# An attention and expert kernel on one core: PSUM banks, the order of rows, transfers and threshold steps rearranged, and products without a use put on TensorE around the boundary of its two programs

## The chip, the core and the metric

The kernel runs on one core of a Trainium2 chip. The metric is the device time of one execution in microseconds (us). The engines of the core are named as the profile names them: PE is TensorE (PEld its weight loads), DVE is VectorE, ACT is ScalarE, POOL is GpSimd, SP is SyncE, which here only starts transfers. Each engine runs its own list of instructions in order; semaphores join them.

## The reference, cut to what matters

```
xn  = layernorm(x)                                   # x: 2 x 4096 x 512, so 8192 rows of 512
qkv = xn @ qkv_w + qkv_b                             # in windows of 64 rows, 16 heads of 32
p   = softmax(q @ k.T / sqrt(32) + rel_bias)         # 64 x 64 for each window and head
att = (p @ v) @ proj_w + proj_b
scores = (xn @ Wg.T).T                               # 8 experts x 8192 rows
top_vals, token_idx = top_k(scores, 1024)            # for each expert
token_w = softmax(top_vals)
h   = silu(xg @ W1.T) * (xg @ W3.T)                  # xg = xn[token_idx], 1024 x 512, hidden 1024
y   = (h @ W2.T) * token_w
out = x + att + scatter_add(y at token_idx)
```

## The kernel before

The kernel is two programs, one after the other. `attention_block` makes layernorm, attention, the gate scores and the choice of 1024 rows for each expert. `expert_block` runs the eight experts. Every large product is made three times over (`split3`, lines 59 to 61: high by high, high by low, low by high parts, each 128 x 128 by 512 columns), and twelve such products make one 128 x 512 result.

The attention program goes over 16 chunks of 512 rows (c = 0 to 15, T = 512, G = 4 groups of four heads, s = 4c + g). Its order is written out by hand for every engine. On PE a chunk is: q and k of group 0, the tiles 0 and 1 of v, pv (line 918) of a group of the chunk before, scores (line 852) of group 0; q and k of group 1, v tiles 2 and 3, pv, scores of group 1; q and k of group 2, `project_out` tile 0 of the chunk before, the gate product of the next chunk (line 832), `project_out` tiles 1 and 2, pv, scores of group 2; `project_out` tile 3, q and k of group 3, pv, scores. Below, out0 to out3 are the four tiles of `project_out`, v0 to v3 those of v, and T0 is the start of a chunk's first q product.

A group's softmax goes round four engines: DVE adds the bias to the scores and takes the maximum (`add_bias`, lines 1203 and 1208), POOL subtracts it (482), ACT takes the exponential (633), DVE sums (1212) and inverts (1216), POOL multiplies (498), DVE turns 32 x 32 blocks (`turn_probs`, 1255), ACT copies (`own_blocks`, 629), SP moves the other blocks (`spread_probs`, 377), and PE reads them in pv. ACT also copies q and k out of PSUM (613 and 638), DVE copies v (`v_part`, 1268).

The next chunk's rows are loaded (`load_x`, 571), normed on DVE (`layernorm_stats`, 1155; `layernorm_apply`, 1174; the square root is POOL's line 468), stored (`keep_xn`, 576), loaded back in another layout (`load_back`, 388) and turned on DVE (`turn_blocks`, 1180); the gate product reads them. In chunks 4 to 9 the five last chunks' rows go the same way ahead of time (the names with `_ahead`: 593, 597, 405, 1185, 838). `finish_rows` (1221) adds `project_out` to the residual rows `x_res`, which `load_res` (588) loads and `store_out` (581) stores.

PSUM has eight banks. Scores take 0 to 3, pv takes 4 and 5, q takes 6 (QB), k takes 7 (KB). v and `project_out` have no banks of their own: they go where `V_BANK` and `P_BANK` say.

Chunks 10 to 14 (`hunt_chunk`) also look for the threshold of each expert, two bits of a float's order at a time in 16 rounds: `search` (1308, then `threshold_float` 1292 and 1293, then three comparisons 1312 and 1313), a product (943) and `take_bits` (1298 to 1304). Chunk 13 chooses (`choose`, 1332), chunk 14 makes places and weights, chunk 15 makes the first expert's list (products 157).

## Time and profile before

| | |
|---|---|
| runs | 2065.02, 2067.38, 2062.08 us, median 2065.02 |
| the profiled execution | 2066.15 us, its span 2064.3 us |
| PE busy in the span | 1961.5 us (95%), mean granted clock 0.977 |
| DVE, ACT, POOL busy | 1185.0, 648.7, 600.9 us |
| chunks 1 to 9 | 68.07 to 600.85 us |
| chunks 10 to 15 | 600.85 to 957.04 us |
| the end of the first program and the start of the second | 957.04 to 991.30 us |
| the experts | 991.30 to 2064.3 us |

The rows of the trace, in a section below, are read like this. A row of the timeline has a start, a duration, engine, line, operation and the names it writes and reads; in brackets stands how long the engine sat idle before it and what ended that. "<-issue" is idle time with no cause that the profile shows. PEclk is the clock that TensorE was granted, 1.00 for 2.4 GHz and 0.50 for 1.2 GHz. Matmuls overlap, so one of 512 columns reads 0.39 us while the next one starts 0.227 us after it, and at half clock reads 0.63 us while the next starts 0.427 us after it.

### The profile page before, as it was taken

What the parts mean: (1) busy time and instruction counts of PE and PEld (TensorE: products, weight loads), DVE (VectorE), ACT (ScalarE), POOL (GpSimd) and SP (SyncE); (2) the same over time, 40 slices, a digit from 0 to 9 for tenths busy, and PEclk for the clock granted to TensorE, in tenths of its full rate; (3) what the DMA queues carried; (4) which work ended last, traced back from release to release, by engine and by line L of the source; (5) the groups of instructions that cost most, each with busy time, mean ns of one, the idle gap of its engine ahead of it and who ended that gap; (6) DMA issues with size and microseconds to landing.
All of it is one profiled execution on the core that took longest, in us unless ns stands there. A gap on an engine that the chain in (4) does not pass through costs nothing.

```text
span 2064.3 us, 39324 instructions
## 1 busy us (share of the span) xinstructions
PE 1961.5 (95%) x16627; PEld 1575.6 (76%) x16627; DVE 1185.0 (57%) x1688; ACT 648.7 (31%) x953; POOL 600.9 (29%) x410
## 2 busy tenths in 40 slices
PE   7899989899998899988899999999999999999997
PEld 5677767677777777776688888888888888888886
DVE  6666668677768898776744544345344543444221
ACT  3333333232333343332333242233332333323221
POOL 1444445444344443454122021211212112102111
PEclk9999999999999999999999999999999999999999
DMA  6333355566542222323444253233532434325311
GB/s 188 111 113 111 105 168 140 140 180 168 146 131 67 58 63 78 84 68 103 154 108 107 81 133 92 55 110 88 128 83 62 126 82 104 91 70 142 61 21 21
DMA packets 170612, 213.63 MB, mean 103 GB/s; under 512 B 31712, under 2 KB 103776, under 8 KB 170464
## 3 DMA queue, kind: packets, MB, share of 16 engines
q1 hardware_dynamic: 124976, 116.12, 20.4%
q0 software_dynamic: 14336, 33.56, 9.1%
q10 hardware_dynamic: 31152, 61.87, 8.7%
q8 instruction: 106, 1.74, 0.4%
q14 instruction: 42, 0.34, 0.1%
HBM read 127.08 MB, written 51.38 MB: 86 GB/s over the span
## 4 chain that ended last, share of the span: by engine, by line
PE 49%; DVE 1%; SPq 1%; ACT 0%; DMA 0%; issue 0%; POOL 0%; POOLq 0%
PE ps_e L59 16%; PE ps_e L60 16%; PE ps_e L61 16%; SPq L197 1%; PE ps_e L157 0%; DMA raw<-in_w 0%; ACT w_hi L1737 0%; DVE w_lo L1848 0%; DVE x_f L145 0%; DVE xn L1854 0%; POOL out_rows L1701 0%; DVE hm L1880 0%; DVE xgt_lo L1859 0%; DVE hot_v L136 0%; ACT x_res L1769 0%
## 5 line engine op out<-in xcount | busy, mean ns | idle before, releaser
L59 PE MATMUL ps_e<-xgt_hi,w_hi 128*128 128x512 f32 x1024 | 404.3, 395 | 7.7 <-DVE xgt_lo L1859 7.7
L61 PE MATMUL ps_e<-xgt_hi,w_lo 128*128 128x512 f32 x1024 | 399.0, 390 | 0.0
L60 PE MATMUL ps_e<-xgt_lo,w_hi 128*128 128x512 f32 x1024 | 399.0, 390 | 0.0
L1880 DVE TENSOR_TENSOR hm<-ps_e,silu 128x512 f32<-128x512 f32 x128 | 88.5, 691 | 457.2 <-PE ps_e L61 456.4
L59 PEld LDWEIGHTS ps_e<-xgt_hi,w_hi 128*128 128x128 f32 x1024 | 192.5, 188 | 46.5 <-DVE xgt_lo L1859 8.4
L1701 POOL DMA_INDIRECT out_rows<-x_res,idx x64 | 100.6, 1572 | 428.1 <-ACT x_res L1769 413.7
L61 PEld LDWEIGHTS ps_e<-xgt_hi,w_lo 128*128 128x128 f32 x1024 | 192.6, 188 | 40.5
L60 PEld LDWEIGHTS ps_e<-xgt_lo,w_hi 128*128 128x128 f32 x1024 | 192.9, 188 | 38.1
L186 POOL DMA_INDIRECT x_in<-xn_rows,idx x64 | 80.1, 1252 | 481.3 <-DVE idx L178 307.5
L59 PE MATMUL ps<-xt_hi,wqk_hi 128*128 128x512 f32 x512 | 209.2, 409 | 4.1 <-DVE v_sb L1268 1.8
L60 PE MATMUL ps<-xt_lo,wqk_hi 128*128 128x512 f32 x512 | 203.4, 397 | 3.9 <-issue 3.9
L61 PE MATMUL ps<-xt_hi,wqk_lo 128*128 128x512 f32 x512 | 202.3, 395 | 0.7 <-issue 0.7
L1757 ACT ACTIVATE h_hi<-hm 128x512 fp32r<-128x512 f32 x128 | 81.0, 633 | 387.7 <-DVE hm L1880 384.8
L59 PE MATMUL ps_e<-w_hi,h_hi 128*128 128x512 f32 x512 | 199.3, 389 | 0.6 <-DVE got L165 0.6
L60 PE MATMUL ps_e<-w_lo,h_hi 128*128 128x512 f32 x512 | 199.2, 389 | 0.0
L61 PE MATMUL ps_e<-w_hi,h_lo 128*128 128x512 f32 x512 | 199.2, 389 | 0.0
L498 POOL TENSOR_TENSOR pn_sb<-p_sb,s_rec 128x1024 f32<-128x1024 f32 x62 | 119.2, 1922 | 260.9 <-DVE s_rec L1216 196.6
L482 POOL TENSOR_TENSOR s_sb<-s_sb,s_max 128x1024 f32<-128x1024 f32 x64 | 122.8, 1919 | 211.5 <-DVE s_max L1208 211.5
L1866 DVE TENSOR_TENSOR h_lo<-hm,h_hi 128x512 fp32r<-128x512 f32 x128 | 88.6, 692 | 94.6 <-ACT h_hi L1757 91.5
L629 ACT ACTIVATE pt<-pn_sb 128x1024 f32<-128x1024 f32 x62 | 65.7, 1060 | 237.2 <-DVE pn_sb L1255 231.1
L1255 DVE STREAM_TRANSPOSE pn_sb<-pn_sb 128x1024 f32<-128x1024 f32 x62 | 77.1, 1243 | 84.3 <-POOL pn_sb L498 83.7
L1769 ACT ACTIVATE x_res<-ps_e,weight 128x512 f32<-128x512 f32 x64 | 43.0, 690 | 251.0 <-PE ps_e L61 251.0
(188 smaller groups left out, 3471.6 us busy)
## 6 DMA issues: line engine op xcount, KB each, us to landing
x_f<-in_w SPq DMA_DIRECT2D x48, 512.0 KB
raw<-in_w SPq DMA_DIRECT2D x48, 512.0 KB
x_res<-in_x ACTq DMA_DIRECT2D x16, 1024.0 KB, 8.7
xn<-x_in SPq DMA_DIRECT2D x256, 64.0 KB, 2.0
pt<-pn_sb SPq DMA_DIRECT2D x248, 64.0 KB
out_rows<-x_res ACTq DMA_DIRECT2D x15, 1024.0 KB
xn_rows<-xt_plain ACTq DMA_DIRECT2D x9, 1024.0 KB, 4.2
x_in<-xn_rows SPq DMA_DIRECT2D x28, 256.0 KB, 4.2
```

Source lines behind the costliest of these rows:

```text
L59: nc.tensor.matmul(out, w_hi, x_hi, start=start, stop=False)
L60: nc.tensor.matmul(out, w_hi, x_lo, start=False, stop=False)
L61: return nc.tensor.matmul(out, w_lo, x_hi, start=False, stop=stop)
L186: nc.gpsimd.indirect_dma_start(out=k.x_in[:, t, :], out_offset=None, in_=xn_rows, in_offset=bass.IndirectOffsetOnAxis(ap=k.idx[par][:, til ...
L482: nc.gpsimd.tensor_tensor(s_sb[:, :, :, :], s_sb[:, :, :, :], s_max[:, :].rearrange("p (t h) -> p t h", t=TT).unsqueeze(3) .to_broadcast([ ...
L498: nc.gpsimd.tensor_tensor(halves_first(pn_sb[:, :]), p_sb[:, :, :, :].rearrange("p t h (j c) -> p (t h) j c", c=QD), s_rec[:, :].unsqueeze ...
L629: nc.scalar.activation(pt[s % 2][:, :, :, :, :].rearrange("p i t h q -> p (i t h q)"), pn_sb[:, :], ACT.Copy).then_inc(pt_own, 1)
L1255: nc.vector.transpose(blocks, blocks).then_inc(pn_turned, 1)
L1701: nc.gpsimd.indirect_dma_start(out=d["out"], out_offset=bass.IndirectOffsetOnAxis(ap=lists.idx[par][:, tile0 + t:tile0 + t + 1], axis=0), ...
L1757: nc.scalar.activation(h_hi[:, m, :], hm[:, m % 2, :], ACT.Copy).then_inc(h_hi_ready, 1)
L1866: v.tensor_tensor(h_lo[:, m, :], hm[:, m % 2, :], h_hi[:, m, :].bitcast(F32), ALU.subtract).then_inc(h_ready, 1)
L1880: v.tensor_tensor(hm[:, m % 2, :], ps[:, 2 * (m % 2) + 1, :], silu[:, m % 2, :], ALU.mult).then_inc(hm_ready, 1)
```

## The change

It has five parts.

1. Banks. `V_BANK` and `P_BANK` become QB, KB, QB, KB. v0 to v3 and out0 to out3 no longer touch the scores' banks 0 and 1. So v tiles wait for the copy of q or k that was in the bank, out0 and out1 likewise, and out2 and out3 wait for `finish_rows` of out0 and out1. Scores wait neither for `v_part` nor for `finish_rows`. What follows in QB or KB (the next q and k) waits for `v_part`.
2. Rows. On DVE `layernorm_stats` goes ahead of `normaliser(s - 1)` and `layernorm_apply` ahead of `v_part(c, 1)`. `turn_blocks` goes ahead of `add_bias(s + 1)`, all of `turn_blocks_ahead` behind it. `gate_rows` goes ahead of `turn_probs(s + 1)`, and `gate_rows_ahead` and `layernorm_stats_ahead` behind the third `finish_rows`. POOL's `layernorm_rstd` goes ahead of `normalise(s - 1)`. PE's `gate_ahead` goes behind out2. In chunks 10 to 14 two of the four `turn_blocks` go behind `take`.
3. Transfers. `load_res`, `keep_xn`, `keep_xn_ahead` and `load_x_ahead` go from ACT's queue to SP's. `load_x` stays on ACT and is issued at the end of the chunk before.
4. Thresholds. The key is kept as the float's own bits, so `threshold_float` (two instructions) is needed once, not in each of 16 rounds and in `choose`, which also loses a copy.
5. Products without a use: 16 behind the last `probs_t` and 12 behind the last `pv`, each 128 x 256, and 26 of 128 x 128 in full float ahead of the first expert. Nothing reads them.

The diff, cut to its core:

```
-        V_BANK, P_BANK, FINAL_BANK = (0, KB, 0, KB), (0, 1, QB, KB), (0, 1, 2, 3)
+        V_BANK, P_BANK, FINAL_BANK = (QB, KB, QB, KB), (QB, KB, QB, KB), (0, 1, 2, 3)
...
                 spread_probs(s - 2)
+                load_res(c - 1)
...
                 if FAR < j <= NCH:
-                    load_back_ahead(j - 1)
+                    keep_xn_ahead(j - 1)
+                if n < FAR:
+                    keep_xn(n)
                 spread_probs(s - 1)
                 if n < NCH:
                     load_back(n)
+                if FAR < j <= NCH:
+                    load_back_ahead(j - 1)
                 spread_probs(s)
+                if j == FAR:
+                    sp.wait_ge(xn0_stored, 2 * 16 * TT * NQ)
+                if FAR <= j < NCH:
+                    load_x_ahead(j)
...
                 subtract_max(s - 1)
-                normalise(s - 1)
                 if n < FAR:
                     layernorm_rstd(n)
+                normalise(s - 1)
...
                 k_part(s + 3, 3)
+                if c + 2 < FAR:
+                    load_x(c + 2)
...
             def project_v(c, t):
-                if t % 2:
-                    pe.wait_ge(k_ready, G * c + t // 2 + 1)
-                elif G * c + t // 2 >= 1:
-                    pe.wait_ge(s_ready, G * c + t // 2)
+                pe.wait_ge(k_ready if t % 2 else q_ready, G * c + t // 2 + 1)
...
                 if t == 0:
                     pe.wait_ge(o_ready, s)
-                    pe.wait_ge(s_ready, s + 2)
-                elif t == 2:
                     pe.wait_ge(q_ready, s + 3)
-                elif t == 3:
+                elif t == 1:
                     pe.wait_ge(k_ready, s + 3)
+                else:
+                    pe.wait_ge(out_ready, TT * c + t - 1)
...
                 pv(s - 2, 2)
-                pe.wait_ge(v_ready, TT * c + 1)
                 slot_read(c, 1)
                 scores(s)
+                pe.wait_ge(v_ready, TT * c + 1)
                 project_q(s + 1, 1)
...
                 lists_of(6)
+                if ahead:
+                    gate_ahead(j - 1)
                 pv(s, 0)
                 lists_of(7)
-                pe.wait_ge(out_ready, TT * (c - 1) + 2)
...
+            def idle_products(n, bank):
+                for _ in range(n):
+                    nc.tensor.matmul(ps[:, bank, 2 * P:4 * P], wqk_hi[:, 0, 0, :], wv_hi[:, 0, 0:2 * P], start=True, stop=True)
...
                 probs_t(s + 3)
+                idle_products(16, OT)
                 pv(s + 3, 3)
+                idle_products(12, PT)
                 pe.wait_ge(o_ready, G * NCH)
...
             def search(i):
-                then(v.scalar_tensor_tensor(cand[:, :], pattern[:, :], 30 - 2 * i, key[:, 0:1].to_broadcast([P, 3]),
-                                            ALU.logical_shift_left, ALU.bitwise_or))
-                threshold_float()
+                then(v.scalar_tensor_tensor((thr if i else cand)[:, :], pattern[:, :], 30 - 2 * i, key[:, 0:1].to_broadcast([P, 3]),
+                                            ALU.logical_shift_left, ALU.bitwise_xor))
+                if i == 0:
+                    threshold_float()
...
-                turn_blocks(c + 1, *range(KC))
+                turn_blocks(c + 1, 0, 1)
                 take(c, 4)
                 if choosing:
                     take_room(SLOT)
                     choose_ties()
+                turn_blocks(c + 1, 2, 3)
...
+            for _ in range(26):
+                nc.tensor.matmul(ps[:, LISTS, 0:P], lists.ident[:, :], lists.ident[:, :], start=True, stop=True)
             expert(0)
```

Three places show what the order becomes. DVE in the first half of chunk 3, before (s_sb is the bias, ot_lo the low part of pv's result, s_sum and s_rec the normaliser, pn_sb the turned probabilities):

```order
133 L1212 TENSOR_REDUCE s_sum<-p_sb 128x16 [waits exp_ready]
134 L1216 RECIPROCAL s_rec<-s_sum 128x16 [waits norm_ready,sum_ready]
135 L1268 TENSOR_TENSOR v_sb<-ps,v_bias 128x512 [waits v_mm,o_mm]
136 L1255 STREAM_TRANSPOSE pn_sb<-pn_sb 128x1024 [waits norm_ready]
137 L1268 TENSOR_TENSOR v_sb<-ps,v_bias 128x512 [waits v_mm]
138 L1155 BN_STATS stats<-x_in 128x6 [waits x_loaded]
139 L1155 BN_STATS stats<-x_in 128x6 x3
140 L1160 BN_AGGR mv<-stats 128x2 [waits stat_ready]
141 L1160 BN_AGGR mv<-stats 128x2 x3
142 L1163 TENSOR_SCALAR veps<-mv 128x4 [waits mv_ready]
143 L1203 TENSOR_TENSOR s_sb<-ps,rel 128x4x4x64 [waits exp_ready,s_mm]
```

and now:

```order
133 L1158 BN_STATS stats<-x_in 128x6 [waits x_loaded]
134 L1158 BN_STATS stats<-x_in 128x6 x3
135 L1163 BN_AGGR mv<-stats 128x2 [waits stat_ready]
136 L1163 BN_AGGR mv<-stats 128x2 x3
137 L1166 TENSOR_SCALAR veps<-mv 128x4 [waits mv_ready]
138 L1215 TENSOR_REDUCE s_sum<-p_sb 128x16 [waits exp_ready]
139 L1219 RECIPROCAL s_rec<-s_sum 128x16 [waits norm_ready,sum_ready]
140 L1271 TENSOR_TENSOR v_sb<-ps,v_bias 128x512 [waits v_mm,o_mm]
141 L1258 STREAM_TRANSPOSE pn_sb<-pn_sb 128x1024 [waits norm_ready]
142 L1177 TENSOR_SCALAR xt_plain<-x_in,mv,rstd 128x4x4x32 [waits rstd_ready]
143 L1177 TENSOR_SCALAR xt_plain<-x_in,mv,rstd 128x4x4x32 x3
144 L1271 TENSOR_TENSOR v_sb<-ps,v_bias 128x512 [waits v_mm]
```

The statistics moved ahead of the normaliser and the norming ahead of the copy of v1. SP's queue over one chunk with rows ahead, before:

```order
109 L377 DMA pt<-pn_sb 32x512 [waits pt_own]
110 L377 DMA pt<-pn_sb 32x512 x3
111 L405 DMA x_f<-xn_rows 32x16x128 [waits xnf_stored]
112 L405 DMA x_f<-xn_rows 32x16x128 x3
113 L377 DMA pt<-pn_sb 32x512 [waits pt_own]
114 L377 DMA pt<-pn_sb 32x512 x3
115 L388 DMA x_in<-xn_rows 32x16x128 [waits xn_stored]
116 L388 DMA x_in<-xn_rows 32x16x128 x3
```

and now:

```order
106 L377 DMA pt<-pn_sb 32x512 [waits pt_own]
107 L377 DMA pt<-pn_sb 32x512 x3
108 L385 DMA x_res<-in_x 128x4x512 [waits out_stored]
109 L394 DMA xn_rows<-xt_f 128x4x512 [waits xnf_ready]
110 L399 DMA xn_rows<-xt_plain 128x4x512 [waits xn_ready]
111 L377 DMA pt<-pn_sb 32x512 [waits pt_own]
112 L377 DMA pt<-pn_sb 32x512 x3
113 L409 DMA xn<-xn_rows 32x16x128 [waits xn_stored]
114 L409 DMA xn<-xn_rows 32x16x128 x3
115 L426 DMA x_f<-xn_rows 32x16x128 [waits xnf_stored]
116 L426 DMA x_f<-xn_rows 32x16x128 x3
```

Three transfers of ACT's stand between the first two spreads now, and the load back of the rows ahead stands behind the load back of the next chunk. PE at the end of the first program, now (before, the two rows of 128x256 and the one of ps_e<-ident are not there):

```order
3419 L897 MATMUL ps<-ident,pn_sb 128x128 [waits ptb_ready,pta_ready,norm_ready]
3420 L897 MATMUL ps<-ident,pn_sb 128x128 x7
3421 L1111 MATMUL ps<-wv_hi,wqk_hi 128x256 x16
3422 L915 MATMUL ps<-pt,v_sb 32x64 [waits o_ready,ptb_ready,pta_ready]
3423 L915 MATMUL ps<-pt,v_sb 32x64 x31
3424 L1111 MATMUL ps<-wv_hi,wqk_hi 128x256 x12
3425 L59 MATMUL ps<-wp_hi,ot_hi 128x512 [waits o_ready]
```

The products stand ahead of the instruction that waits, so they run while it would wait.

## Rows read from the trace of the kernel before

**Rows 1.** Stretches: us, busy us (instructions) of each engine, PEclk, DMA share, GB/s.

```profile
68.07:600.85 532.78, 497.50 (x6455) 384.79 (x6449) 374.98 (x541) 162.46 (x216) 241.74 (x158) 0.96 0.48 139
600.85:957.04 356.19, 328.77 (x4282) 264.12 (x4276) 287.73 (x457) 129.73 (x215) 156.10 (x98) 0.96 0.27 78
...
991.30:2064.30 1073.00, 1061.62 (x5051) 870.69 (x5049) 452.50 (x598) 322.38 (x475) 172.80 (x121) 1.00 0.37 90
```

**Rows 2.** Chunks, the same view: 1, 6, 7, 11 and 13.

```profile
68.07:123.75 55.68, 52.73 (x718) 41.58 (x713) 36.84 (x51) 18.01 (x24) 26.19 (x17) 1.00 0.37 116
...
356.11:421.68 65.57, 58.23 (x727) 43.95 (x721) 45.99 (x69) 18.06 (x24) 27.38 (x18) 0.92 0.52 148
...
421.68:479.40 57.72, 55.72 (x727) 42.82 (x721) 45.54 (x69) 18.13 (x24) 27.41 (x18) 0.97 0.59 168
...
661.89:722.80 60.91, 55.66 (x706) 44.68 (x704) 52.79 (x95) 23.99 (x44) 25.52 (x16) 0.94 0.26 71
...
782.37:842.45 60.08, 55.94 (x721) 44.84 (x716) 50.25 (x87) 21.40 (x36) 24.64 (x16) 0.94 0.26 72
```

**Rows 3.** Waits of PE in chunks 1 to 15: total us, times, longest.

```profile
PE ps L852 <- DVE x_res L1221: 15.7, 5, 4.4
PE ps L832 <- DVE xt_plain L1180: 13.7, 6, 4.8
PE ps L59 <- ACT k_sb L638: 13.3, 8, 1.9
```

**Rows 4.** Timeline of chunk 7 up to the turned rows.

```profile
421.64 0.53 ACTq L571 DMA_DIRECT2D x_in<-in_x  x1
...
424.63 0.68 DVE L1273 TENSOR_TENSOR ot_lo<-ps,ot_hi 128x512 fp32r<-128x512 f32 x1
...
427.82 1.22 DVE L1212 TENSOR_REDUCE s_sum<-p_sb 128x16 f32<-128x1024 f32 x1 [2.51 <-ACT p_sb L633]
...
432.07 1.91 POOL L498 TENSOR_TENSOR pn_sb<-p_sb,s_rec 128x1024 f32<-128x1024 f32 x1 [5.38 <-DMA pt<-pn_sb]
...
435.75 2.45 DVE L1155 BATCH_NORM_STATS2 stats<-x_in 128x6 f32<-128x512 f32 x4
...
441.79 3.12 DVE L1174 TENSOR_SCALAR xt_plain<-x_in,mv,rstd 128x512 f32<-128x512 f32 x4
...
444.94 0.37 ACTq L576 DMA_DIRECT2D xn_rows<-xt_plain  x1
...
444.98 0.50 PE L59 MATMUL ps<-wv_hi,xt_hi 128*128 128x512 f32 x1 [1.89 <-ACT k_sb L638]
...
457.01 2.49 DVE L1180 STREAM_TRANSPOSE xt_plain<-x_in 128x512 f32<-128x512 f32 x4 [2.52 <-DMA x_in<-xn_rows]
```

**Rows 5.** Timeline of chunk 6: the gate product.

```profile
399.63 1.94 PE L832 MATMUL ps<-xt_plain,wg 128*32 128x512 f32 x8 [4.78 <-DVE xt_plain L1180]
```

**Rows 6.** Timeline of chunk 11, DVE and PE around scores of group 2.

```profile
701.36 1.75 DVE L1293 SCALAR_TENSOR_TENSOR thr<-cand,flip 128x3 int32<-128x3 int32 x1
...
703.14 2.88 DVE L1312 TENSOR_SCALAR x_f<-x_f,thr 128x512 bf16<-128x512 f32 x2
...
706.61 0.68 DVE L1221 TENSOR_TENSOR x_res<-ps,x_res 128x512 f32<-128x512 f32 x1
...
709.07 1.28 PE L852 MATMUL ps<-k_sb,q_sb 32*64 32x64 f32 x64 [4.39 <-DVE x_res L1221]
```

**Rows 7.** Line 1293: duration ns min/median/max, first and last start.

```profile
L1293 DVE SCALAR_TENSOR_TENSOR thr<-cand,flip x17: 161/163/1746, 620.6 to 809.1; 128x3 int32<-128x3 int32 x17
```

**Rows 8.** Timeline of the boundary: PE.

```profile
973.10 0.85 PE L918 MATMUL ps<-pt,v_sb 64*32 64x64 f32 x64 [2.20 <-ACT pt L620]
...
975.36 0.80 PE L59 MATMUL ps<-wp_hi,ot_hi 128*128 128x512 f32 x1 [1.41 <-DVE ot_lo L1273]
...
988.58 0.79 PE L59 MATMUL ps_e<-xgt_hi,w_hi 128*128 128x512 f32 x1 [7.73 <-DVE xgt_lo L1859]
```

**Rows 9.** Transfers of 60 to 960 us: count, KB each, median us to landing.

```profile
x_in<-in_x ACTq DMA_DIRECT2D x5, 1024.0 KB, 7.8
```

90 lines of the change are left out of this document (38 added, 52 removed).

## The prediction, made before the changed kernel ran

> **What bounds the kernel now.** I read the stretches first, then the chunks, then PE's waits, then the timeline around the waits. The experts run from 991.30 us to the end with PE busy in 1061.62 of 1073.00 us at full clock, and the change only puts products ahead of them [rows 1]. So all that can move lies ahead of 991 us. There PE is the engine that the others wait for, but it has holes. In chunks 1 to 9 it is busy 497.50 of 532.78 us, in chunks 10 to 15 328.77 of 356.19 [rows 1]: 35.3 and 27.4 us idle. A part of the busy time is work at half clock as well. Chunk 1, all of it at clock 1.00, has 52.73 us of PE work [rows 2]. Nine of these are 474.6 us, the five gate products ahead add 1.06 us each, and 17.6 of the 497.5 us are left: that is what 1.2 GHz costs there. Six times 52.7 from 328.8 leaves 12.6 us in chunks 10 to 15. So holes and half clock together are 93 us, the most the change could give but for the boundary.
>
> Three waits make most of the holes [rows 3]: scores behind `finish_rows` (15.7 us, 5 times, in the chunks from 10 on), the gate product behind `turn_blocks` (13.7 us, 6 times) and v3 behind the copy of k (13.3 us, 8 times, once in each chunk from 1 to 9 but one). The change takes away all three as they stand. What counts is which wait ends last in its place.
>
> **Chunks 1 to 9, first half of a chunk.** I follow chunk 7, T0 = 421.68, and count from T0. Now the rows are loaded from 421.64 (T0+0) [rows 4]; the statistics begin at 435.75 (T0+14.1), so `add_bias` of group 0 behind them is late, and with it the maximum, the subtraction, the exponential and the copy of k: v3 starts at 444.98 (T0+23.3) after 1.89 us of waiting. In the change the statistics stand behind `ot_lo`, whose instruction ends at T0+3.6 [rows 4]. They can't begin sooner than that, and not before the rows are there. The load goes out up to a microsecond sooner and a median one lands after 7.8 us [rows 9], beside another megabyte that now starts later. So they begin between T0+3.6 and T0+7; I take T0+5.5, between the two. They take 3.0 us. The normaliser had its exponential at 427.82 (T0+6.1) [rows 4], needs 1.5 us, and now ends at T0+8.1 to 11.5 (10.0). POOL's multiplication began at T0+10.4 since it waited 5.38 us for the spread [rows 4]; the spread is now ahead of the residual's load, so POOL goes by the normaliser, 1.9 us, to T0+12.0. The turning of the probabilities takes 1.25, `layernorm_apply` 3.12, the copy of v1 0.65: T0+17 (15.2 to 18.6). k of group 1, next in bank KB, wants it at T0+15.5. **New wait one: 0 to 3.1 us, I take 1.4.** From the copy of v1 on, `add_bias`, maximum, subtraction, exponential and copy of k take 6.1 us as before; v3 starts at T0+23.1 (21.3 to 24.7), where it is 23.3 now. So the wait of 1.9 us is cut into two of 1.4 and about 0.6, and nothing is won but the clock: chunk 7 has 55.72 us of busy time [rows 2] where 52.73 and 1.06 would do. The 1.9 us over are v3's, whose products ran at 1.2 GHz behind the hole.
>
> **Second half of a chunk.** From the store of the normed rows (444.94) to the turned ones (457.01) the way is 12.1 us [rows 4]. The norming now ends at T0+16.4, so they are back at T0+28.5, and DVE has copied v3 at about T0+26.6. `turn_blocks` (2.5), `add_bias` and maximum (2.4) and `ot_lo` (0.7) now stand ahead of out0, which gets its input at T0+34.1. PE wants it 10 us behind v3's start (v3, pv, scores, q, k): at T0+33.1. **New wait two: about 0.9 us.** For that the gate product waits for nothing, where it waited 4.78 us in chunk 6 [rows 5] and 13.7 in all. out1 and out2 find k copied and out0 finished with 0.5 to 2 us to spare. In chunks 4 to 8 `layernorm_stats_ahead` (3.0 us) now stands ahead of `add_bias` of group 2, and its rows can't be loaded before `turn_blocks_ahead`, now late in the chunk: between 0 and 2 us each, 0.6 taken. Sum of the nine chunks: idle 9 x 2.9 + 5 x 0.6 = 29 us, and 4 us of fetches and spreads stay: 33 for 35.3, so **2 us**. The new holes are each below 1.9 us, the size behind which chunk 7 ran v3 slowly; a hole of 1.04 us in chunk 1 left the clock at 1.00 [rows 2]. So nearly all of the 17.6 us of half clock goes; I take **17**. Bounds for the stretch: -4 (each new wait at its upper end, clock as now) and +38.
>
> **Chunks 10 to 15.** In chunk 11 the last search ahead of `finish_rows` has an instruction of three numbers (line 1293) that takes 1.75 us, and two comparisons that take 2.88 [rows 6]; line 1293 has a median of 0.16 us [rows 7]. They stretch while POOL works. `finish_rows` of out0 runs at 706.61 to 707.3, of out1 0.6 us behind the next turning, and scores start at 709.07 after 4.39 us [rows 6]. In the change out2 (2.73 us) waits for out0's, and scores come 3.6 us behind it. With `finish_rows` where it is, scores would be later by 1.8 us. But each search loses two instructions, between 0.35 us (two at 0.17) and some 2.5 us (two behind a POOL instruction), and the last two searches of the chunk add up. I take 2.8 us sooner: scores 1.0 us sooner, and 0.7 us less waiting ahead of the small products. With that 2 us for each of the chunks 10 to 12, **6 us**. The hole stays above 3 us, so does its half clock. Chunk 13's choice loses three such instructions, in the trace 1.2 us each beside POOL's residual, which held up the copy of v3 and through it PE by 1.75 us, and a later wait of 2.2 us with its half clock: **5 us** of its 60.08 against 52.7 [rows 2]. Chunk 15: scores no longer wait for v0, **1 us**. Together 12, between 0 and 20.
>
> A row here speaks of a cost that may not leave. The comparisons right behind line 1293 are themselves stretched, 2.88 us for the two [rows 6]. If they are what would wait next, the search gets only the 0.17 us of each instruction back: `finish_rows` comes 1.3 instead of 2.8 us sooner, and these three chunks lose what they won: 2030 becomes 2036. The Trainium skill says so (SBUF — State Buffer, section on the two separate sides): a VectorE instruction that uses the port pair shared with GpSimd blocks fully until GpSimd's instruction ends. That is a rival below.
>
> **The boundary.** PE waits 2.20 us, then 1.41, then 7.73 [rows 8]; between the last two, out0 to out3's last 12 products run from 975.36 at 0.427 us each, and the first seven of the experts too. A product of 256 columns is half of 0.227 us: 16 are 1.8 us, 12 are 1.4, hidden in the first two holes. The 26 are of full float like the gate product, whose four, of 512 columns and side by side, take 1.06 us at full clock: with 128 columns one takes 0.27 us at most, all 7.0 us, hidden in 7.73. If the clock stays up, 12 x 0.2 and 7 x 0.2 us go: **4 us**. At half clock the 26 take up to 14 us and hold the experts up by up to 6.
>
> **The sum.** 2 + 17 + 12 + 4 = 35. The profiled execution took 2066.15 us (span 2064.3), so 2031.2; the median of the runs is 1.1 lower, so 2030.
>
> **Rivals.**
> 1. *The holes only move* (0.20). The new wait for v1's copy, out0's and out2's wait are near their upper ends and the clock drops behind them. Against it: each is short by the rows. Then chunks 1 to 9 give 5, 10 to 15 give 4, the boundary 4: 2053.
> 2. *The rows come late* (0.06). All of the first half now hangs on the load of x: each us past T0+5.5 costs one in each of nine chunks. At T0+9.4 the 35 us are gone; at T0+10.5, as late as with two other megabytes in flight, the kernel stands at 2030 + 45 = 2075, slower.
> 3. *The blocked time passes on* (0.14), as said: 2036.
> 4. *The products don't keep the clock* (0.10): the 26 delay the experts by up to 6 us, say 4, instead of winning 4: 2038.
> 5. *More goes* (0.10). If the load lands at T0+3.6, wait one and most of two vanish too: 9 x 2 us more, 2012.
>
> The forecast has 0.40. The range of 2010 to 2056 takes in the first rival and the fifth, and leaves out the second and the tails. About 0.3% (6 us) can be told from no change. Faster by more than that has 0.90, within it 0.05, slower 0.05.
>
> **What would show it.** In the changed profile: scores behind `finish_rows`, the gate product behind `turn_blocks` gone from PE's waits; products with wqk behind a copy of v about 12 us in all; wp products behind `ot_lo` about 8 us; out2 behind `finish_rows` 3 to 4 us in each of three chunks; PEclk 1.00 in most of chunks 1 to 9; PE full from 970 us on with no product at 0.63 us. Wrong would be: statistics that wait for the load past T0+7, or a clock that falls behind holes of 1.4 us.

## The result: 2006.7 us, 58.7 less, and more than the forecast had

| | before | changed |
|---|---|---|
| median of the runs shown | 2065.41 us (2062.08 to 2067.38) | 2006.71 us (2006.31 to 2008.94) |
| ratio | | 0.972, 95% interval 0.9703 to 0.9736 |
| span of the profiled execution | 2064.3 us | 2004.5 us |
| PE busy, mean granted clock | 1961.5 us, 0.977 | 1946.2 us, 0.992 |

The forecast was 2030, with 2010 to 2056 as its range. The direction was right and the size was not: the time lies 3 us below the range.

The stretches of the changed kernel come first, cut at the same places in the program as [rows 1], but for the last cut, which is the first product of the experts here (930.25 us, and 988.58 us before). The columns are those of [rows 1].

```profile
67.07:554.59 487.52, 481.65 (x6454) 376.57 (x6449) 368.51 (x541) 160.41 (x216) 241.95 (x158) 1.00 0.53 152
554.59:901.85 347.26, 324.06 (x4281) 260.03 (x4275) 276.63 (x426) 130.15 (x215) 156.10 (x98) 0.98 0.28 80
901.85:930.25 28.40, 25.80 (x342) 22.02 (x337) 21.65 (x28) 9.23 (x14) 12.16 (x9) 1.00 0.43 137
930.25:2004.50 1074.25, 1062.90 (x5056) 871.56 (x5056) 455.02 (x601) 322.81 (x475) 173.50 (x123) 1.00 0.37 91
```

For the kernel before, the last two with the same cut (PE's time only):

```profile
957.04:988.58 31.54, 18.99 (x262) 0.83 0.39 122
988.58:2064.30 1075.72, 1064.34 (x5056) 0.99 0.37 91
```

| stretch | before | changed | gain | forecast |
|---|---|---|---|---|
| up to chunk 1 | 68.07 | 67.07 | 1.0 | 0 |
| chunks 1 to 9 | 532.78 | 487.52 | 45.3 | 19 |
| of it PE busy (half clock) | 497.50 | 481.65 | 15.9 | 17 |
| of it PE idle | 35.28 | 5.87 | 29.4 | 2 |
| chunks 10 to 15 | 356.19 | 347.26 | 8.9 | 12 |
| boundary and experts | 1107.26 | 1102.65 | 4.6 | 4 |

So one term holds the whole miss: the idle time of PE in chunks 1 to 9. I had written 33 us for it in the changed kernel, and it is 5.9. (One execution is not exact to the microsecond. `idle_only`, an experiment below whose program is that of the kernel before in these chunks, takes 539.8 us for them where the row of the kernel before has 532.8; three experiments with the changed kernel's program in them take 487.2 to 487.6.) The waits of PE in these chunks are now (total us, times, longest), where [rows 3] had 13.7 and 13.3 us:

```profile
PE ps L59 <- issue: 2.7, 2, 2.3
PE ps L59 <- ACT k_sb L648: 1.2, 5, 0.3
PE ps L60 <- issue: 0.9, 1, 0.9
```

None of the new waits that I had put there shows: no product with wqk waits for a copy of v (12 us were said), none with wp waits for `ot_lo` (8 us).

**Chunk 7 of the changed kernel** answers [rows 4]; T0 is 386.87. Line numbers have moved a little: statistics 1158, applying 1177, copy of v 1271, turning 1183.

```profile
385.26 0.39 ACTq L602 DMA_DIRECT2D x_in<-in_x  x1
...
392.62 2.47 DVE L1158 BATCH_NORM_STATS2 stats<-x_in 128x6 f32<-128x512 f32 x4 [0.22 <-DMA x_in<-in_x]
...
399.20 1.25 DVE L1258 STREAM_TRANSPOSE pn_sb<-pn_sb 128x1024 f32<-128x1024 f32 x1 [1.47 <-POOL pn_sb L529]
400.37 1.88 DVE L1177 TENSOR_SCALAR xt_plain<-x_in,mv,rstd 128x512 f32<-128x512 f32 x4
402.16 0.69 DVE L1271 TENSOR_TENSOR v_sb<-ps,v_bias 128x512 f32<-128x512 f32 x1
...
402.27 0.36 SPq L399 DMA_DIRECT2D xn_rows<-xt_plain  x1
...
402.93 0.47 PE L59 MATMUL ps<-xt_hi,wqk_hi 128*128 128x512 f32 x1
...
413.62 2.48 DVE L1183 STREAM_TRANSPOSE xt_plain<-x_in 128x512 f32<-128x512 f32 x4
...
418.37 0.68 DVE L1276 TENSOR_TENSOR ot_lo<-ps,ot_hi 128x512 fp32r<-128x512 f32 x1
```

Read it against the prediction's walk, in us from T0. The statistics begin at 5.75 (I had 5.5). The turned probabilities are done at 13.6 (13.2). Applying takes 1.88 us, where I had 3.12 from [rows 4], so it ends at 15.4 and the copy of v1 at 16.0 (17). PE asks for that bank at 16.06 (15.5): it comes 0.1 us too late to wait. The turned rows are not waited for either: `turn_blocks` starts as the copy of v3 ends, at 26.7 (28.5), and `ot_lo` is done at 32.2 (34.1), where out0 starts (33.1). Not every link was shorter: the first ones ended 0.3 to 0.4 us later than I had. But applying took 1.2 us less and PE asked 0.6 us later, and together that is the 1.4 us of the first forecast wait. out0 was asked for 0.9 us sooner than I had, and its input was there 1.9 us sooner.

**Chunks 10 to 12** have the new hole that the prediction named. The waits stand ahead of out1 and out2, here in chunk 10 (the next eight products start 0.33 to 0.59 us apart, at half clock):

```profile
592.59 0.50 PE L59 MATMUL ps<-wp_hi,ot_hi 128*128 128x512 f32 x1 [1.68 <-ACT k_sb L648]
...
598.61 0.79 PE L59 MATMUL ps<-wp_hi,ot_hi 128*128 128x512 f32 x1 [2.96 <-DVE x_res L1224]
```

And what `finish_rows` stands behind on DVE, with POOL's rows beside it:

```profile
593.68 3.61 DVE L1320 TENSOR_SCALAR x_f<-x_f,thr 128x512 bf16<-128x512 f32 x2
593.70 1.91 POOL L529 TENSOR_TENSOR pn_sb<-p_sb,s_rec 128x1024 f32<-128x1024 f32 x1 [2.83 <-DVE s_rec L1219]
595.56 5.33 POOL L538 TENSOR_TENSOR xt_lo<-xt_plain,xt_hi 128x512 fp32r<-128x512 f32 x4
597.21 0.73 DVE L1321 TENSOR_SCALAR_CACHE_REDUCE x_f<-x_f,thr 128x512 bf16<-128x512 f32 x1
...
597.87 0.68 DVE L1224 TENSOR_TENSOR x_res<-ps,x_res 128x512 f32<-128x512 f32 x1
```

**The boundary** answers [rows 8]: the idle products fill the holes, and the first product of the experts starts 0.06 us behind the end of `xgt_lo`.

```profile
919.43 0.50 PE L59 MATMUL ps<-wp_hi,ot_hi 128*128 128x512 f32 x1
...
924.12 6.04 PE L1840 MATMUL ps_e<-ident 128*128 128x128 f32 x52 [1.67 <-PEq L208]
...
927.63 2.56 DVE L1866 TENSOR_TENSOR xgt_lo<-xn,xgt_hi 128x512 fp32r<-128x512 f32 x4
930.25 0.50 PE L59 MATMUL ps_e<-xgt_hi,w_hi 128*128 128x512 f32 x1
```

### The profile page after: what moved, and what is told of

It reads as the page before. It is cut to its first block, busy times and chain, and to the rows that moved or that the text cites. A ratio compares the mean times of both kernels' runs of the same rounds, so it can differ in the third digit from the quotient of the medians.

```text
span 2004.5 us, 39470 instructions
## 1 busy us (share of the span) xinstructions
PE 1946.2 (97%) x16707; PEld 1569.4 (78%) x16707; DVE 1166.6 (58%) x1657; ACT 647.1 (32%) x953; POOL 599.5 (30%) x410
## 3 DMA queue, kind: packets, MB, share of 16 engines
q1 hardware_dynamic: 143456, 152.82, 26.7%
## 4 chain that ended last, share of the span: by engine, by line
PE 51%; DVE 1%; ACT 1%; SPq 0%; DMA 0%; issue 0%; POOL 0%; POOLq 0%
PE ps_e L59 17%; PE ps_e L61 17%; PE ps_e L60 17%; PE ps_e L157 1%; SPq L197 0%; DMA raw<-in_w 0%; ACT w_hi L1742 0%; DVE w_lo L1855 0%; DVE x_f L145 0%; DVE xn L1861 0%; POOL out_rows L1706 0%; DVE hm L1887 0%; DVE xgt_lo L1866 0%; DVE hot_v L136 0%; ACT x_res L1774 0%
## 5 line engine op out<-in xcount | busy, mean ns | idle before, releaser
L59 PE MATMUL ps<-wp_hi,ot_hi 128*128 128x512 f32 x256 | 106.5, 416 | 15.2 <-DVE x_res L1224 9.7
```

The costliest lines, as they stand in the source:

```text
L59: nc.tensor.matmul(out, w_hi, x_hi, start=start, stop=False)
```

## The experiments

Fifteen kernels, each the changed kernel or the kernel before with one or two edits. "Changed" is 2006.7 us. Each was run beside the kernel before, and the ratio given is to that. The intervals of the ratios are 0.4 to 1.2% wide, 4 to 13 us each way, and no experiment ran beside the changed kernel itself, so a difference from "changed" that is smaller than that rests on the waits and stretches of the profiles. The stretches of an experiment are cut where a chunk starts, as before.

### Two links made longer

`apply_plus`:

```diff
...
                 dve.wait_ge(rstd_ready, c + 1)
+                for t in ((0, 1) if c >= 2 else ()):
+                    nc.vector.tensor_reduce(idle_sum[:, 2 * c + t:2 * c + t + 1], v_bias[:, :], AX.X, ALU.add)
```

> The changed kernel with two sums over the bias of v (about 0.6 us each on DVE, results unused) ahead of layernorm_apply in chunks 1 to 8: what the applying would take if it were stretched as in the kernel before (3.12 instead of 1.88 us). In the changed kernel the copy of v1 ends 1.5 to 1.8 us ahead of the product of k that waits for its bank in chunks 1 to 4, and 0.06 to 0.4 us ahead in chunks 5 to 9. Theory A, the gain is there because this chain comes out just short: about 1 us of new waiting in each of chunks 5 to 8 and none in 1 to 4, so 4 us and up to 4 more of half clock, 2011 (2010 to 2015). Rival, the chain has slack that the profile doesn't show: 2006 to 2008.

Measured: 2012.6 us (ratio 0.9741, 0.9696 to 0.9786), 5.9 us more. The interval holds the changed kernel's 0.972, but all four runs lie above all four of the changed kernel, and chunks 1 to 9 take 496.0 us instead of 487.5. The sums run in nine chunks, 1 to 9, not in eight as the expectation has it (18 sums, of 0.66 us each at the median). The products with wqk now wait for the copy of v, 3.8 us in 5 times, the longest 1.1.

`load_late`:

```diff
                 o_hi_part(s - 3, 1)
+                if c + 1 < FAR:
+                    load_x(c + 1)
                 own_blocks(s - 2)
...
-                if c + 2 < FAR:
-                    load_x(c + 2)
```

> The changed kernel with the load of x for the next chunk issued where the kernel before issues it, behind the first copy of a chunk on ACT, about 2 us later than in the changed kernel. Theory A: in chunks 5 to 8, where the statistics now start just as the rows land (T0+5.4 to 5.7), each loses about 2 us, in chunks 1 to 4 at most 0.5, so 8 to 10 us and some half clock: 2016 (2013 to 2022). Rival, the rows have time to spare: 2006 to 2009.

Measured: 2014.4 us (0.9748, 0.9702 to 0.9794), 7.7 us more. Again all four runs lie above the changed kernel's, and chunks 1 to 9 take 6.4 us more. The number was met, the reason was not. The rows below are the start of the statistics in chunks 2 and 5 of the changed kernel, of `load_late` and of `apply_plus`, in this order:

```profile
123.03 2.47 DVE L1158 BATCH_NORM_STATS2 stats<-xn 128x6 f32<-128x512 f32 x4 [0.33 <-DMA xn<-in_x]
282.54 2.46 DVE L1158 BATCH_NORM_STATS2 stats<-x_in 128x6 f32<-128x512 f32 x4
```

```profile
127.36 2.47 DVE L1157 BATCH_NORM_STATS2 stats<-xn 128x6 f32<-128x512 f32 x4 [2.04 <-DMA xn<-in_x]
289.16 2.46 DVE L1157 BATCH_NORM_STATS2 stats<-x_in 128x6 f32<-128x512 f32 x4
```

```profile
125.00 2.48 DVE L1159 BATCH_NORM_STATS2 stats<-xn 128x6 f32<-128x512 f32 x4 [1.72 <-DMA xn<-in_x]
286.83 2.46 DVE L1159 BATCH_NORM_STATS2 stats<-x_in 128x6 f32<-128x512 f32 x4
```

With the late load, the statistics wait for the rows in chunks 1 to 4 only (3.2, 2.0, 2.9 and 1.8 us), and 6.6 us are lost by chunk 5. Behind it they wait for nothing (no bracket), and 0.2 us more are lost by chunk 9, where they start at 511.90 us against 505.11. In chunks 5 to 9 DVE is not back from the work for the rows ahead of time (`layernorm_apply_ahead`) until T0+5.4, so the load has time there. I had it the other way round. `apply_plus` loses 4.3 us by chunk 5, where I had expected none, and 3.4 more by chunk 9 (8.4 us of span in the profiled execution, 5.9 by the medians).

`plus_and_late` has both edits:

> The changed kernel with both links of the rows' way made as long as the prediction took them: the load of x at its old place on ACT, and 1.2 us of sums on DVE ahead of layernorm_apply. Theory A, the prediction's 2030 was wrong in these links' lengths and not in its picture: with slack used up by the one, the other costs its full 1.2 us in each of eight chunks, and the two cost more than the 5.9 and 7.7 us they cost alone: 2022 to 2030. Rival, they only add up or overlap, and what the prediction missed lies elsewhere (how soon PE asks, the way to DRAM and back): 2015 to 2021.

Measured: 2022.6 us (0.9788, 0.9763 to 0.9812), 15.9 us more, where the two alone give 13.6. That the two cost more together than alone is not shown: in chunks 1 to 9 they cost 14.4 us together and 8.5 and 6.4 alone. With the two links at the lengths that I had taken, the kernel comes 7 us short of my 2030, not 23. In chunks 1 to 9 themselves, where I had 513.8 us, it takes 501.9 and the changed kernel 487.5: the two links are 14 of the 26 us there, and 12 are left. Its chunks 1 to 9, and their waits:

```profile
65.53:567.40 501.87, 485.75 (x6450) 1.00 0.51 148
```

```profile
PE ps L59 <- DVE v_sb L1273: 6.1, 7, 1.3
PE ps L59 <- issue: 3.4, 2, 2.2
PE ps L59 <- ACT k_sb L649: 3.3, 13, 0.3
PE ps L59 <- DVE ot_lo L1278: 1.5, 2, 1.3
```

These are waits of the prediction. The one for the copy of v1 has half its size, the one for `ot_lo` a fifth. The copy of v1 ends at T0+16.6 to 17.1 in the seven chunks that wait for it, where I had T0+17. But PE asks for its bank at T0+15.8 in chunks 1 to 4 and at T0+16.3 in the later ones, where I had 15.5 for all nine.

`apply_plus4` has four sums instead of two.

> The changed kernel with four sums (2.6 us) instead of two (1.3 us, 2012.6) ahead of layernorm_apply in chunks 1 to 8. Theory A, with the slack gone each further microsecond costs one in each of eight chunks, and the holes are now long enough for half clock behind some: 10 to 16 us more than with two, 2023 to 2029. Rival, the cost stays in proportion: 2017 to 2020.

Measured: 2023.0 us (0.9799, 0.9772 to 0.9826), 10.4 us more than with two, for 1.3 us in each of nine chunks, 11.8 in all. By the medians the first two sums cost half of that and the next two nearly all of it. The profiled executions don't say so: chunks 1 to 9 take 8.5 us more with the first two and 7.6 more with the next two (487.5, 496.0 and 503.6 us). So whether a further microsecond costs a whole one is open. PE waits 11.3 us for the copy of v, 9 times, the longest 2.2 us, and its clock in these chunks is still 1.00.

### The applying back beside POOL's subtraction

`apply_behind`:

```diff
                 turn_probs(s - 1)
-                if n < FAR:
-                    layernorm_apply(n)
                 v_part(c, 1)

                 add_bias(s, 0)
                 o_lo_part(s - 2, 2)
+                if n < FAR:
+                    layernorm_apply(n)
```

> The changed kernel with layernorm_apply back behind ot_lo of group 2, where POOL's subtraction runs beside it. Theory A: it takes 3.1 us again instead of 1.9; the normed rows are stored at T0+20 instead of T0+15.4, come back 10 us later at T0+30, and turn_blocks, add_bias and ot_lo stand ahead of out0, which waits 3 us in each of nine chunks: 27 us, and half clock behind these holes on top, 2035 to 2048. Rival, the rows come back with time to spare and only the order of the copies mattered: 2006 to 2012.

Measured: 2062.9 us (against before 0.9984, 0.9964 to 1.0003): one call moved by three lines, and nearly all of the gain is gone. Chunks 1 to 9 take 53.1 us more than in the changed kernel: 38.6 us more of idle PE, and 14.6 us more for the same products, some of them at half clock (the mean granted clock there is 0.97). The rows that I had in mind are there, applying at 3.12 us and out0 behind `ot_lo`, and one that I had not, a blocked queue. Timeline of chunk 4, DVE, SP's queue and POOL:

```profile
257.43 1.91 POOL L513 TENSOR_TENSOR s_sb<-s_sb,s_max 128x1024 f32<-128x1024 f32 x1 [5.36 <-DVE s_max L1211]
257.86 3.12 DVE L1177 TENSOR_SCALAR xt_plain<-xn,mv,rstd 128x512 f32<-128x512 f32 x4
...
261.01 0.39 SPq L399 DMA_DIRECT2D xn_rows<-xt_plain  x1
261.44 3.25 SPq L377 DMA_DIRECT2D pt<-pn_sb  x4
...
266.30 1.90 POOL L529 TENSOR_TENSOR pn_sb<-p_sb,s_rec 128x1024 f32<-128x1024 f32 x1 [6.96 <-DMA pt<-pn_sb]
...
272.58 2.49 DVE L1183 STREAM_TRANSPOSE xt_plain<-xn 128x512 f32<-128x512 f32 x4 [2.53 <-DMA xn<-xn_rows]
```

SP's queue stands at the store of the normed rows until 261.01 us, and the spread behind it, whose data was turned at 253.3, goes out at 261.44. Waits of PE in chunks 1 to 9:

```profile
PE ps L59 <- DVE ot_lo L1276: 28.5, 8, 5.2
PE ps L915 <- DMA pt<-pn_sb: 7.9, 8, 2.2
```

To see what the blocked queue is worth, `apply_behind_free` also puts the store behind the spread:

```diff
-                if n < FAR:
-                    keep_xn(n)
                 spread_probs(s - 1)
+                if n < FAR:
+                    keep_xn(n)
```

> The kernel with layernorm_apply behind ot_lo of group 2 (2062.9), with one more edit: on the SP queue the store of the normed rows stands behind the spread of the probabilities instead of ahead of it. In the trace of that kernel the spread goes out at 261.4 us, right behind the store, though the probabilities were turned at 253.3, and POOL waits 7.0 us for it. Theory A, the blocked queue is the smaller part: the waits for the spread (7.9 us in all) and some half clock go, out0 behind ot_lo (28.5 us) stays, 2050 to 2057. Rival, the blocked queue is what makes that kernel slow: 2015 to 2040.

Measured: 2067.1 us (against before 1.002, 0.9995 to 1.0046), no better. Neither theory had that.

```profile
PE ps L59 <- DVE ot_lo L1276: 42.1, 8, 7.1
```

The waits for the spread are gone, and out0's wait is 13.6 us longer. In chunks 1 to 4 the turning of the rows starts at T0+30.2 to 30.6 with the blocked queue and at T0+30.4 to 30.9 with the free one. So PE comes to out0 sooner and meets rows that are no sooner: the way norm, store, load back, turn sets that moment, and what is freed beside it moves the wait. Why out0 lost 13.6 us and not only the 7.9 us that were freed was not followed.

### The transfers back on ACT

`act_transfers` gives `load_res`, `keep_xn`, `keep_xn_ahead`, `load_x_ahead` and `load_x` their old places on ACT:

```diff
...
                 k_part(s + 1, 1)
+                if n < FAR:
+                    keep_xn(n)
                 own_blocks(s)
                 o_hi_part(s - 1, 3)
...
+                if FAR <= j < NCH:
+                    load_x_ahead(j)
                 q_part(s + 2, 2)
...
```

> The changed kernel with its five transfers back on ACT at their old places; DVE's and POOL's order, the banks, the searches and the idle products stay changed. Theory A, the early rows are worth nothing while the store of the normed rows stands behind the copy of k on ACT: it goes out at T0+22 instead of T0+15.4, the turned rows come 6 us later, and now add_bias and ot_lo stand behind them, so out0 waits about 6 us in each of nine chunks, half clock behind each, and the later load costs its 8 us: 2070 to 2085, slower than the kernel before. Rival, the order of DVE is what counts and the queue is free: 2012 to 2030.

Measured: 2115.1 us (against before 1.026, 1.0198 to 1.0321), 30 us worse than my worse theory. ACT and PE in chunk 6:

```profile
411.27 0.58 ACT L645 ACTIVATE ot_hi<-ps 128x512 fp32r<-128x512 f32 x1
424.12 0.38 ACTq L583 DMA_DIRECT2D x_f<-in_x  x1
424.60 0.69 ACT L613 ACTIVATE q_sb<-ps,q_bias 128x512 f32<-128x512 f32 x1 [12.75 <-DVE xt_f L1190]
425.43 0.77 PE L59 MATMUL ps<-wp_hi,ot_hi 128*128 128x512 f32 x1 [9.02 <-ACT q_sb L613]
```

The load ahead of time waits until `x_f` has been turned. The changed order of DVE turns it later, behind `add_bias` and `ot_lo`. So ACT stands still for 12.75 us with the copy of q behind the transfer, and in the new banks out0 waits for that copy: four waits of 9.0 us, 36.5 us with a small fifth one. out0 waits 20.6 us more for `ot_lo`, and the wqk products 16.5 us for copies of v. So the new order of the rows can't be taken without the move of the transfers: with both, chunks 1 to 9 are 45 us shorter than before, and without the second they are 61 us longer and the whole kernel is 50 us slower than before. The other half, the transfers moved in the old order, was not run, nor was this kernel with the old banks, in which out0 doesn't wait for the copy of q.

### The banks

`old_banks` is the changed kernel with the old banks and waits:

```diff
-        V_BANK, P_BANK, FINAL_BANK = (QB, KB, QB, KB), (QB, KB, QB, KB), (0, 1, 2, 3)
+        V_BANK, P_BANK, FINAL_BANK = (0, KB, 0, KB), (0, 1, QB, KB), (0, 1, 2, 3)
...
```

> The changed kernel with the banks of v and of the output products (and PE's waits for them) as in the kernel before; the order of DVE, the transfers, the searches and the idle products stay changed. Theory A, the rows and transfers carry the gain and the banks are worth nothing or less: in chunks 1 to 9 every old wait would be met in time by the changed kernel's trace (add_bias of group s+1 ends at T0+30.3, out0 wants it at T0+32.2), so no difference there; in chunks 10 to 12 out1 no longer waits for k (1.1 to 1.7 us) nor out2 for finish_rows (3.0 us), and scores wait about 2.5 us for finish_rows of out1 instead: 2 to 3.5 us sooner in each, so 1995 to 2002. Rival, the banks carry a good part of the gain: slower, 2012 to 2030, with scores behind finish_rows at 3 us or more again in the chunks from 10 on.

Measured: 1998.3 us (0.9684, 0.9655 to 0.9713), 8.4 us less than changed. The banks are a loss. In chunks 10 to 15 (the same wait was 15.7 us in the kernel before):

```profile
PE ps L852 <- DVE x_res L1228: 9.3, 4, 3.2
```

Chunks 1 to 9 take 487.2 us, as with the new banks (487.5). The loss is all in chunks 10 to 15, which take 8.5 us less with the old banks, 4.9 us of idle PE and 3.6 of busy time. The wait above stands in place of 9.7 us of out2 for the same `finish_rows` and 4 us of out1 for the copy of k.

`banks_only` is the kernel before with the changed banks and nothing else.

> The kernel before with the changed banks of v and of the output products and PE's waits for them (with the wait of the gate products for the scores that the banks need, and the second gate product behind out2), and nothing else of the change. Theory A, the banks only trade waits: in chunks 1 to 9 nothing (the copy of v1 ended 0.4 to 2.7 us ahead of k), in chunks 10 to 15 the 8 us that the old banks won in the changed kernel are lost: 2070 (2064 to 2078). Rival, the banks take away the waits for finish_rows and these are worth something by themselves: 2045 to 2060.

Measured: 2075.9 us (1.0063, 1.0038 to 1.0089), 13.5 us more than the kernel before in the same comparison, between 8 and 18 by the interval. v and out1 wait 27.5 us for the copy of k (17 times) where 13.3 were waited. The gate product waits 20.4 us where it waited 13.7, but that proves nothing: it waits 23.7 in `idle_only`, which has the old banks. Chunks 10 to 15 take 4.3 us more, and chunks 1 to 9 6.1 us more, which is no more than two executions of the same chunks differ. Both runs say that the banks cost time, about 8 us in the changed kernel; where the 13 us go in the kernel before is not shown.

### Where `finish_rows` stands

`finish_first`, in the chunks that search:

```diff
+                finish_rows(c - 1, 0)
                 prepare(c, 5)
-                finish_rows(c - 1, 0)
                 turn_probs(s + 1)
```

> The changed kernel with one line moved in the chunks that search (10 to 13): finish_rows of out0 ahead of the last search's comparisons, which take 4.3 us beside POOL's work, instead of behind them. Theory A, the comparisons are what the out2 product waits for: the three waits of 2.96 to 3.00 us go, and about 1 us of half clock in each: 1995 to 1999. Rival, the time passes on to the next wait (the turned probabilities, k or the count of the search): 2003 to 2007.

Measured: 1994.3 us (0.9668, 0.9638 to 0.9698), 12.4 us less than changed. out2's waits fall from 9.7 to 3.9 us, and chunks 10 to 15 take 10.7 us less, 5.6 of it busy time. No products at half clock are left in chunks 10 to 14, where the changed kernel has them behind two of the waits of 3 us.

`old_banks_first` has the old banks and both `finish_rows` ahead of the comparisons.

> Both of the above: the changed kernel with the old banks, and in the chunks that search finish_rows of out0 and of out1 ahead of the last search's comparisons. Theory A, nothing of the output products is then waited for in chunks 10 to 12: out1, out2 and scores start as PE comes to them, 4.5 us sooner in each than in the changed kernel, and half clock goes with the holes: 1990 to 1996. Rival, the next wait takes their place: 1998 to 2005.

Measured: 1992.1 us (0.9649, 0.9619 to 0.9679). Chunk 11, where the changed kernel takes 57.81 us:

```profile
612.40:667.00 54.60, 52.92 (x719) 1.00 0.28 78
```

What is left there is a wait for the last search's hits, 1.5 us in this chunk and 5.6 us in the four such waits of chunks 10 to 12. `count_late` moves those products behind q of group 3:

```diff
...
-                hunt(c, 5)
                 pe.wait_ge(out_ready, TT * (c - 1) + 3)
                 project_q(s + 3, 3)
+                hunt(c, 5)
```

> The kernel with the old banks and finish_rows of out0 and out1 first (1992.1), with the small products that count the last search's hits behind q of group 3 instead of ahead of it. Theory: PE's wait for the hits ahead of them (5.6 us in four chunks) goes and nothing waits in its place, since the count is wanted by the next chunk: 1986 to 1989. Rival, the next search starts later and holds up what stands behind it on DVE: 1991 to 1996.

Measured: 1993.4 us (0.966, 0.960 to 0.971). No gain; 3.5 us of that wait stay and k's and the issue's grow. `finish_first`, `old_banks_first` and `count_late` can't be told apart. All three beat both kernels of this study.

### The thresholds

`old_thresholds` builds each threshold as before:

```diff
-                then(v.scalar_tensor_tensor((thr if i else cand)[:, :], pattern[:, :], 30 - 2 * i, ...
+                then(v.scalar_tensor_tensor(cand[:, :], pattern[:, :], 30 - 2 * i, ...
-                if i == 0:
-                    threshold_float()
+                threshold_float()
...
```

> The changed kernel with the searches' thresholds as in the kernel before: each round builds the integer candidate and turns it into a float with two more instructions, and the choice with three more. Theory of the prediction: chunk 13 loses about 5 us, chunks 10 to 12 up to 2 us each in the wait for finish_rows: 2013 to 2018. Rival, the comparisons beside POOL take what the instructions give back: 2007 to 2010.

Measured: 2019.0 us (0.978, 0.9751 to 0.981), 12.3 us more. Chunks 10 to 13 take 63.2, 62.2, 61.4 and 58.1 us where the changed kernel takes 60.7, 57.8, 60.0 and 53.8. In chunk 11 `finish_rows` of out0 is back at T0+44.7, where the kernel before has it, and out2 waits 4.22 us. The rival of the passed-on time is refuted as to the total. It is there in part: line 1320's comparisons have a mean of 895 ns where the same ones had 670 in the kernel before, 7.2 us more in 32 of them, and with the old thresholds 668 again. They were not all in PE's way.

### The boundary

`no_idle` is the changed kernel without the three loops of products.

> The changed kernel without its three groups of idle products, all else the same. Theory A, the products keep the clock: the last twelve products of out0 to out3 take about 0.427 us each again instead of 0.23, and the first experts' products too, so the execution is about 4 us longer than the changed kernel's 2006.7, near 2011 (the boundary was 31.5 us from the last scores to the first expert product before and is 27.5 now). Rival, they only fill holes and the 4 us came from the work around them: 2006 to 2008, with the first expert product still 27.5 us behind the last scores.

Measured: 2009.4 us (0.9729, 0.9683 to 0.9776). The medians differ by 2.7 us, which the interval can't tell; the profile shows the mechanism:

```profile
932.64 0.80 PE L59 MATMUL ps_e<-xgt_hi,w_hi 128*128 128x512 f32 x1 [7.73 <-DVE xgt_lo L1862]
```

Behind it thirteen products of the first expert start 0.427 us apart, and so do the last twelve of out0 to out3 ahead of it. (The expectation's 27.5 us was cut one block of scores later than its 31.5: cut alike, the boundary is 31.5 us before and 28.4 in the changed kernel, and the rest of the 4.6 us lies in the first expert.)

`idle_only` is the kernel before with the products alone.

> The kernel before with the idle products alone. Theory A, as in the changed kernel: out0 to out3's last twelve products and the experts' first dozen at 0.23 us instead of 0.43: 4 to 5 us less than before, 2060 to 2061 where before has 2065. Rival, the gain at the boundary came with the rest: 2065.

Measured: 2061.0 us (0.9981, 0.9962 to 1.0), 4.4 less than before in the same comparison. Taking the products out costs 2.7 us, putting them in gives 4.4, and the rows show full clock with them and half clock without. The profiled executions say it best, from the end of chunk 15 to the end of the program: 1106.4 us (before) and 1107.9 (`no_idle`) without the products, 1101.8 (changed) and 1101.7 (`idle_only`) with them, 4.6 to 6.2 us. So the 4 us stand, though neither comparison of the medians alone could tell them from nothing.

## Why the prediction was right in its direction and wrong in its size

**Half clock in chunks 1 to 9 (17): right in size, by a reason that the rows don't bear.** 15.9 us of busy time went, and PEclk reads 1.00 over the stretch. I had reasoned from the length of one hole: 1.9 us, behind which chunk 7 ran slowly, against holes below it. But the kernel before has a hole of the same length in chunk 1, and the products behind it start 0.23 us apart, at full clock. `apply_plus4` has a longer one with nothing slow behind it:

```profile
91.21 0.50 PE L59 MATMUL ps<-wv_hi,xt_hi 128*128 128x512 f32 x1 [1.88 <-ACT k_sb L638]
```

```profile
417.89 0.50 PE L59 MATMUL ps<-xt_hi,wqk_hi 128*128 128x512 f32 x1 [2.17 <-DVE v_sb L1274]
```

In the changed kernel a hole of 2.33 us in chunk 8 has eight products at half clock behind it. So the length of one hole alone doesn't say whether the clock falls. What else counts was not tried. The prediction had 33 us of holes in the stretch; the most that ran at a mean clock of 1.00 is 18.8 us, in `apply_plus4`. The size came out right, and in part by luck.

**Idle time in chunks 1 to 9 (2): wrong, and the whole miss.** The step that failed is the pair of new waits, 1.4 us for the copy of v1 and 0.9 us for `ot_lo` in each of nine chunks, with the 0.6 us of v3 behind the first. The changed kernel has neither of the two, and 5.9 us of idle PE instead of 33. What I had for each wait, what `plus_and_late` has (the links at my lengths) and what the changed kernel has:

| us in chunks 1 to 9 | forecast | plus_and_late | changed |
|---|---|---|---|
| k of group 1 behind the copy of v1 | 12.6 | 6.1 | 0 |
| v behind the copy of k (forecast for v3 only) | 5.4 | 3.3 | 1.2 |
| out0 behind `ot_lo` | 8.1 | 1.5 | 0 |
| `add_bias` behind the statistics ahead | 3 | 0 | 0 |
| fetches and spreads ("issue" in the rows) | 4 | 4.4 | 3.6 |

The terms that failed, as the prediction put them:

1. "`layernorm_apply` 3.12". That duration came from a place where POOL's subtraction runs beside it, and the change moved it to a place where POOL has just finished. There it takes 1.88. `apply_plus` gives 5.9 us for this alone by the medians, 8.5 in the stretch.
2. "So they begin between T0+3.6 and T0+7; I take T0+5.5", for nine chunks. In chunks 1 to 4 they begin at T0+3.6 to 3.9, my lower end; in 5 to 9 at T0+5.4 to 5.7, for DVE's own work and not for the load (chunk 7, the one that I had followed, waits 0.22 us for it). I had multiplied chunk 7 by nine. In chunks 1 to 4 the copy of v1 ends 1.5 to 1.8 us ahead of PE. `load_late`, which starts them there 1.4 to 2.8 us later, costs 7.7 us.
3. "From the store of the normed rows (444.94) to the turned ones (457.01) the way is 12.1 us". In chunk 7 it is at most 11.3 us now, since `turn_blocks` waits for no transfer there; in chunk 2, where it waits 0.58 us, the way is 12.0. In `plus_and_late`, with the norming as late as I had it, the way is at most 11.3 us in six chunks, and out0 waits 1.5 us in all where I had 8.1. So the way varies, and I had taken one of its longer values for every chunk. No run changed that way alone.
4. "0.6 taken" for the statistics ahead in five chunks: there is no such wait in the changed kernel, nor in the four with longer links.
5. "k of group 1, next in bank KB, wants it at T0+15.5". In the changed kernel PE asks at T0+15.6 in chunks 1 to 4 and at T0+16.1 to 16.2 in chunks 5 to 7 and 9.

Points 1 and 2 were tried: together they are 16 of the 23 us by the medians, and 14 of the 26 us of the stretch. The other 12 us of the stretch (17 us less idle time than I had, 5 us more busy time) lie in points 3 to 5, by the table and the rows; they were not tried one by one.

Behind the five stands one habit. Each new wait was a difference of two sums of five to eight links, near zero, and I took one middle value above zero for all nine chunks. A difference of 1 us that is uncertain by 1.5 us means that some chunks wait and others have time to spare, and the forecast had no chunk with time to spare. The rows said so: chunks 1 and 7 differ by the work for rows ahead, and the same walk from T0+3.6 ends the copy of v1 at T0+15.1 even with 3.12 us of applying, ahead of PE.

**Chunks 10 to 15 (12): 8.9.** I had the thresholds at 15.5 us (2.8 and 0.7 in each of three chunks, 5 in chunk 13), and `old_thresholds` gives 12.3. I had the banks at 4.4 us of loss (1.8 in three chunks, less 1 in chunk 15), and `old_banks` gives 8.4. In the stretch itself they are 13.3 and 8.5. Of the 8.9 some 4 to 5 came with the rest of the change in these chunks, for which I had no term and which was not tried alone. `finish_rows` of out0 in chunk 11 came 2.85 us sooner in its chunk, I had 2.8. out2 waited 2.96 to 3.00 us in three chunks, I had 3 to 4. The missing term is out1, which in the new banks stands in KB and waits for the copy of k: 1.68, 1.09 and 1.25 us in chunks 10 to 12 and 1.17 in chunk 14, where I had nothing. [rows 3] could not show it, but the list of `P_BANK` did.

**The boundary (4): 4.6** with the experts' first products, and the 26 products took 6.04 us where my bound was 7.0.

**The rivals.** Holes that only move (2053): the new waits in chunks 1 to 9 did not come, and no clock fell behind them. Rows that come late (2075): no, but late rows do cost time: `load_late` has the load itself later, and `apply_behind` and `act_transfers` have the normed rows later and end at 2063 and 2115. Blocked time passed on (2036): seen in part, not in the total. Products that don't keep the clock (2038): they do. "More goes" (2012) came nearest. Its mechanism, rows that are there at T0+3.6, holds in chunks 1 to 4 and not in chunk 7, where the shorter applying did the work. I gave it 0.10 and let the range end 2 us below it, and that end rested on one cause of a shorter way where there were several.

## What to carry to other kernels

A duration belongs to its neighbours: before an instruction's time is carried to its new place, look at what the other engines do beside it there. Where a new wait is a small difference of long sums, work it out for each kind of chunk, let it be zero where the slack is negative, and let the range reach to "none of them waits". And a wait that vanishes or a queue that is freed can be worth nothing while another way sets the same point, as in `apply_behind_free`: look for that other way first.

## What the runs showed of the hardware

In these rows a `tensor_scalar` of DVE from SBUF to SBUF that meets a multiplication or subtraction of POOL ends only behind POOL's instruction. The four applyings of one chunk, once beside POOL's subtraction (`apply_behind`) and once alone (changed; columns: shortest, median, longest in ns, first and last start):

```profile
L1177 DVE TENSOR_SCALAR xt_plain<-xn,mv,rstd x4: 534/534/1753, 257.9 to 260.4; 128x512 f32<-128x512 f32 x4
```

```profile
L1177 DVE TENSOR_SCALAR xt_plain<-x_in,mv,rstd x4: 510/546/547, 400.4 to 401.7; 128x512 f32<-128x512 f32 x4
```

Only one of the four is long, and it ends 0.27 us behind POOL's end at 259.34. The Trainium skill says this (SBUF — State Buffer, section on the two separate sides): the shared port pair is locked for a whole instruction and the loser blocks fully. This case agrees: the meeting costs 1.2 us here. The two comparisons of chunk 10 above each met another POOL instruction and took 2.21 and 1.48 us, where the median of their kind is 0.49. In the prediction I used the rule for the comparisons and did not think of it for the applying, whose 3.12 us had the same cause.

A transfer's wait blocks the engine that issues it: 12.75 us of ACT without work, with a copy behind it that PE waited for.
